# The second expert stage of a one-core language tower: from all eight experts of every token to the two chosen experts of each sequence

## The reference, cut to what matters

```python
def _L1_ffn_ref(x, Wr, br, W1, b1, W2, b2, gamma, beta):
    logits = jnp.mean(x, axis=1) @ Wr + br                # (64 sequences, 8 experts)
    routing_weights = jax.nn.softmax(logits, axis=-1)
    ...                                                   # scaled by capacity, softmax again
    top_w, top_i = jax.lax.top_k(rw_tok, 2)
    top_w = jax.nn.softmax(top_w, axis=-1)
    h = gelu(jnp.einsum('nd,edf->enf', xf, W1) + b1[:, None, :])      # 64 -> 128
    y = jnp.einsum('enf,efd->end', h, W2) + b2[:, None, :]            # 128 -> 64
    w_dense = jnp.zeros((N, E), x.dtype).at[jnp.arange(N)[:, None], top_i].add(top_w)
    out = jnp.einsum('ne,end->nd', w_dense, y).reshape(B, S, D)
    out = _layer_norm(out + x, gamma, beta)
```

## Time and profile before

| | before |
|---|---|
| median of 3 runs | 6802.49 us (6799.26 to 6812.74) |
| the profiled execution's own time | 6807.38 us |
| its span, first to last instruction | 6805.7 us |
| busy over the span: PE, DVE, ACT, POOL | 5514.7, 5229.1, 2711.6, 1975.4 us |
| granted TensorE clock, mean | 0.905 of full speed |

### The profile page before, as it was taken

The page is one execution under the profiler, slowest core; times in us unless marked ns, Lnnn a source line. Parts: engine busy times, 40 slices in busy tenths (PEclk is TensorE's granted clock), DMA queues, the critical chain, the costliest instruction groups (busy, mean ns, idle before and its releaser), DMA issues. The chain is left out here.

```text
span 6805.7 us, 109689 instructions
## 1 busy us (share of the span) xinstructions
PE 5514.7 (81%) x41602; PEld 3465.6 (51%) x41668; DVE 5229.1 (77%) x8911; ACT 2711.6 (40%) x4310; POOL 1975.4 (29%) x1937
## 2 busy tenths in 40 slices
PE   5659968958828999992399999999940989599998
PEld 3552256642215666662387878778830368433332
DVE  7878987877878888872288888888863577677776
ACT  3534433433425666661144444444420432233332
POOL 0010010010017830004777777777746010100000
PEclk8879989979969999995699999999975989699999
DMA  0000000002111000001122222222210000000001
GB/s 16 1 6 1 25 17 15 16 11 64 44 42 12 20 9 2 2 8 38 17 44 41 45 40 44 41 45 40 44 24 7 1 3 3 17 1 1 1 1 25
DMA packets 152318, 141.75 MB, mean 21 GB/s; under 512 B 71746, under 2 KB 136419, under 8 KB 150051
## 3 DMA queue, kind: packets, MB, share of 16 engines
q1 hardware_dynamic: 98462, 115.20, 5.8%
q0 software_dynamic: 53376, 20.06, 3.4%
q10 hardware_dynamic: 12, 0.39, 0.0%
HBM read 62.80 MB, written 38.09 MB: 15 GB/s over the span
## 5 line engine op out<-in xcount | busy, mean ns | idle before, releaser
L2888 PE MATMUL edges_bank<-part_room,hot_room 128*128 128x512 f32 x7168 | 1641.5, 391 | 223.5 <-DVE hot_room L2979 190.3
L2888 PEld LDWEIGHTS edges_bank<-part_room,hot_room 128*128 128x128 f32 x7168 | 1347.6, 188 | 517.4 <-issue 190.7
L2876 POOL DMA_INDIRECT XT<-gat_node_table,edges_idx x1152 | 1200.8, 1042 | 463.7 <-issue 460.7
L2909 ACT COPY XT<-edges_bank 128x512 f32<-128x512 f32 x896 | 524.0, 600 | 943.2 <-PE edges_bank L2888 939.4
L2997 DVE COPY_PREDICATED XT<-edges_tabs_p,XT 128x1024 f32<-128x1024 int32 (+3 forms) x896 | 632.9, 706 | 41.4 <-DVE edges_tabs_p L2971 7.4
L2979 DVE TENSOR_SCALAR hot_room<-edges_lanes,edges_nodes 128x512 fp32r<-128x512 f16 x896 | 395.1, 502 | 149.0 <-issue 73.1
L1005 ACT ACTIVATE expd_act_out<-expd_hp 128x1024 f32<-128x1024 f32 x256 | 262.2, 1024 | 525.9 <-PE expd_hp L927 525.9
L1041 DVE TENSOR_TENSOR expd_act_out<-expd_act_out,expd_h 128x1024 f32<-128x1024 f32 x256 | 312.7, 1221 | 185.9 <-ACT expd_act_out L1005 185.8
L1459 ACT ACTIVATE GT<-attc_sc,attc_nm 128x256 f32<-128x256 f32 x1024 | 400.4, 481 | 36.3 <-DVE attc_nm L1525 36.3
L1473 ACT ACTIVATE GT<-attc_sct 128x1024 f32<-128x1024 f32 x256 | 262.4, 1025 | 326.2 <-PE attc_sct L1393 325.5
L1524 DVE TENSOR_REDUCE attc_mx<-attc_sc 128x4 f32<-128x1024 f32 x256 | 313.3, 1224 | 86.9 <-PE attc_sc L1382 86.8
(11 more groups left out here) (774 smaller groups left out, 9895.6 us busy)
## 6 DMA issues: line engine op xcount, KB each, us to landing
edges_lanes<-gat_places SPq DMA_DIRECT2D x224, 128.0 KB, 3.1
gat_states<-GT SPq DMA_DIRECT2D x32, 768.0 KB
XT<-gat_node_table,edges_idx POOLq DMA_INDIRECT x1152
XT<-XT SPq DMA_DIRECT2D x32, 256.0 KB
XT<-XT SPq DMA_DIRECT2D x64, 128.0 KB
XT<-XT SPq DMA_DIRECT2D x128, 64.0 KB
gat_starts<-nodes_zeros SPq DMA_DIRECT2D x4, 1088.0 KB, 8.0
attb_q<-attb_rows SPq DMA_DIRECT2D x256, 2.0 KB
```

What stands on the lines that cost most here:

```text
L2876: nc.gpsimd.indirect_dma_start(out=rows[:, k, c, :], out_offset=None, in_=q.t_table, in_offset=bass.IndirectOffsetOnAxis(ap=idx[:, k, c:c ...
L2888: m = nc.tensor.matmul(banks[t % BANKS][:], hot[:, (k * GROUPS + j) % 2, b, t, :], parts[:, p, b].rearrange("p u c -> p (u c)"), start=b = ...
L2909: nc.scalar.copy(fetched[:, (k * GROUPS + j) % 2, t].rearrange("p u c -> p (u c)"), banks[t % BANKS][:]).then_inc(fetched_in, 1)
```

## The change

`route_sequences`, `ExpertTables` and `experts` are replaced in this block by one stage, `sequence_experts`. In "atta" SyncE builds a table in DRAM, `expert_pairs`, with a block of 128 rows of 384 floats for each ordered pair (a, c) of experts: W1 of a, W2 of a, W1 of c, W2 of c (12.6 MB, 48 DMAs of 256 KB, with rows of 512 bytes for W1 and 256 bytes for W2). In the new stage the router ends in an index for each sequence; GpSimd fetches 128 rows of 1536 bytes (196 KB) for one sequence with one indirect DMA, up to 6 sequences ahead. For each of 64 sequences TensorE does 4 hidden products of 128 columns, ScalarE two Gelus of 128 x 256, VectorE scales the two W2 by the weights (128 x 128), TensorE does 4 output products, ScalarE moves the sum with the mixed bias, TensorE turns it, and VectorE adds it to `X` (128 x 128). Two slots of the sort stand behind each scaling, so that the 125 are spent in 63 iterations.

The core of the diff:

```diff
-    with Stage(nc, "expb_in") as kept:
-        tables = ExpertTables(nc, kept, I["L1_ffn_W1"], I["L1_ffn_W2"], I["L1_ffn_b1"], I["L1_ffn_b2"])
-        route_sequences(nc, g, "routb", I["L1_ffn_Wr"], I["L1_ffn_br"], 8, ahead=tables)
-        experts(nc, g, "expb", tables, target=g.X, hide=HIDDEN["expb"])
+    sequence_experts(nc, g, "expb", pairs, I["L1_ffn_Wr"], I["L1_ffn_br"], I["L1_ffn_b1"], I["L1_ffn_b2"], g.X, HIDDEN["expb"])
...
+    def sync(self, sp):                                        # PairTable; called in attn0 ahead of the sort's slots
+        E = self.E
+        rows = self.table.rearrange("(a c p) (s f) -> a c p s f", a=E, c=E, s=2)
+        for e in range(E):
+            for half in range(2):
+                d = slice(half * D, half * D + D)
+                source = bc(self.W1[e], 1, E)
+                sp.dma_start(rows[e, :, d, 0, 0:P].rearrange("c d f -> d c f"), source).then_inc(self.built, 16)
+                sp.dma_start(rows[:, e, d, 1, 0:P].rearrange("a d f -> d a f"), source).then_inc(self.built, 16)
+            source = bc(self.W2[e], 1, E)
+            sp.dma_start(rows[e, :, :, 0, P:P + D].rearrange("c p f -> p c f"), source).then_inc(self.built, 16)
+            sp.dma_start(rows[:, e, :, 1, P:P + D].rearrange("a p f -> p a f"), source).then_inc(self.built, 16)
...
+                for b in range(B):                             # GpSimd, NB = 6
+                    if b >= NB:
+                        pool.wait_ge(used, b - NB + 1)
+                    nc.gpsimd.indirect_dma_start(
+                        out=chosen[:, b % NB, :], out_offset=None, in_=pairs.table,
+                        in_offset=bass.IndirectOffsetOnAxis(ap=idx[:, b:b + 1], axis=0)).then_inc(gathered[b % NB], 16)
...
+                for i in range(B + 3):                         # TensorE
+                    if i < B:
+                        hidden(i)
+                    if 0 <= i - 2 < B:
+                        out(i - 2)
+                    if 0 <= i - 3:
+                        turn_back(i - 3)
...
+                    for e in range(2):                         # ScalarE, hide_units
+                        m = nc.scalar.activation(hid[:, b % NH, e, :].rearrange("p (a t) -> p a t", a=TPB), hp[b % 2][:, :, e * P:(e + 1) * P], ACT.Gelu, bias=sel[:, e, b:b + 1])
...
+                    nc.scalar.activation(yT[:, b % 2, :], yp[b % 2][:, 0:P], ACT.Identity, bias=sel[:, 2, b:b + 1]).then_inc(y_moved, 1)
...
+                for i in range(B + 3):                         # VectorE, SLOT_RATE = 2
+                    if i < B:
+                        scale(i)
+                    while done < hide and done < (i + 1) * SLOT_RATE:
+                        g.order.vector(v)
+                        done += 1
+                    if 0 <= i - 3:
+                        add(i - 3)
```

More of the change, by code:

```diff
@@ L1090, in _, with attn0 @@
                 sp.wait_ge(stored, 64)
-def attn0(nc, g, I):
+def attn0(nc, g, I, pairs):
     scale = D ** -0.5
@@ L2109, in route_sequences, with sequence_experts @@
+def sequence_experts(nc, g, name, pairs, Wr, br, b1, b2, target, hide):
+    E = pairs.E
+    NB, NH = 6, 3
+    SLOT_RATE = -(-hide // B)
     capacity = float(-(-TOKENS * 5 // (4 * E)))
+    halves = [slice(0, D), slice(D, P)]
     with Stage(nc, name) as st:
         w, bias = st.sb("w", [P, E]), st.sb("bias", [B, E])
+        b1s, b2s = st.sb("b1", [E, P]), st.sb("b2", [E, 2, D])
+        rev = st.sb("rev", [B, E])
         mean = st.sb("mean", [P, B])
-        rw, load, hot, tmp, gt = (st.sb(n, [B, 1, E]) for n in ("rw", "load", "hot", "tmp", "gt"))
@@ L2114, in route_sequences @@
[L2114 to L2122, removed]
@@ L2123, in route_sequences @@
-        gates = GateSplit(nc, g, st, E, rest[:])
+        rw, load, tmp = (st.sb(n, [B, 1, E]) for n in ("rw", "load", "tmp"))
+        hots = st.sb("hots", [B, 3, E])
+        mx, rs, best1, best2, r1, r2, w2e = (st.sb(n, [B, 1]) for n in ("mx", "rs", "best1", "best2", "r1", "r2", "w2e"))
+        vals, diag = st.sb("vals", [B, 3]), st.sb("diag", [B, 3, B])
+        idx = st.sb("idx", [P, B], I32)
+        hotT, sel = st.sb("hotT", [E, 3, B]), st.sb("sel", [P, 3, B])
+        chosen = st.sb("chosen", [P, NB, PAIR])
@@ new lines, in sequence_experts @@
+        hid = st.sb("hid", [P, NH, 2, S])
+        yT = st.sb("yT", [P, 2, P])
+        spread, misc = st.ps("spread", [P, 3, B]), st.ps("misc", [P, 512])
+        small = misc[:, 0:2 * E].rearrange("p (n e) -> p n e", n=2)
+        turned_p = misc[0:E, 128:128 + 3 * B].rearrange("e (n b) -> e n b", n=3)
+        sel_p = misc[:, 320:320 + 3 * B]
+        hp = [st.ps(f"hp{n}", [P, 2, 512]) for n in range(2)]
+        yp, yt = [st.ps("yp", [P, 512]), misc], st.ps("yt", [P, 512])
+        names = ("loaded", "made", "own", "mean_ready", "product", "probs_ready", "shifted", "exped", "gap_ready", "gap_exped",
+                 "vals_ready", "spread_full", "hots_turned", "idx_ready", "hotT_ready", "sel_full", "sel_ready",
+                 "scaled", "hp_full", "hid_full", "used", "y_moved", "y_turned", "y_added")
@@ L2124, in route_sequences @@
+        (loaded, made, own, mean_ready, product, probs_ready, shifted, exped, gap_ready, gap_exped,
+         vals_ready, spread_full, hots_turned, idx_ready, hotT_ready, sel_full, sel_ready,
+         scaled, hp_full, hid_full, used, y_moved, y_turned, y_added) = (st.sem(n) for n in names)
+        gathered = [st.sem(f"gathered{n}") for n in range(NB)]
         with nc.Block() as block:
-            parts = {}
             @block.sync
             def _(sp):
-                sp.dma_start(w[0:D, :], Wr).then_inc(loaded, 16)
-                sp.dma_start(w[D:P, :], Wr).then_inc(loaded, 16)
+                for half in halves:
+                    sp.dma_start(w[half, :], Wr).then_inc(loaded, 16)
@@ L2131, in _ @@
                 sp.dma_start(bias[:], br.partition_broadcast(B)).then_inc(loaded, 16)
-                ahead.sync(sp)
+                sp.dma_start(b1s[:], b1).then_inc(loaded, 16)
+                for n in range(2):
+                    sp.dma_start(b2s[:, n, :], b2).then_inc(loaded, 16)
+                for _ in range(hide):
+                    g.order.sync(sp)
+            @block.gpsimd
+            def _(pool):
+                nc.gpsimd.iota(rev[:], pattern=[[-1, E]], base=E, channel_multiplier=0,
+                               allow_small_or_imprecise_dtypes=True).then_inc(made, 1)
+                pool.wait_ge(pairs.built, 16 * pairs.BUILDS)
+                pool.wait_ge(idx_ready, 1)
+                for b in range(B):
[4 more added lines that the diff above has]
+                        in_offset=bass.IndirectOffsetOnAxis(ap=idx[:, b:b + 1], axis=0)).then_inc(gathered[b % NB], 16)
@@ L2134, in _ @@
             @block.tensor
             def _(pe):
-                pe.wait_ge(loaded, 48)
+                pe.wait_ge(loaded, 96)
                 pe.wait_ge(mean_ready, 1)
@@ L2140, in _ @@
                 nc.tensor.matmul(small[0:B, 1, :], g.ones[0:B, 0:B], rw[:, 0, :], start=True, stop=True).then_inc(product, 1)
[L2141 to L2182, removed]
+                pe.wait_ge(vals_ready, 1)
+                nc.tensor.matmul(spread[:], g.ones[0:B, :], diag[:], start=True, stop=True).then_inc(spread_full, 1)
+                for n in range(3):
+                    m = nc.tensor.transpose(turned_p[:, n, :], hots[:, n, :], g.ident[0:B, 0:B])
+                m.then_inc(hots_turned, 1)
+                pe.wait_ge(hotT_ready, 1)
@@ new lines, in _, with hidden @@
+                nc.tensor.matmul(sel_p[:, 0:2 * B], b1s[:], hotT[:, 0:2, :], start=True, stop=True)
+                nc.tensor.matmul(sel_p[:, 2 * B:], b2s[:].rearrange("e n d -> e (n d)"), hotT[:, 2, :],
+                                 start=True, stop=True).then_inc(sel_full, 1)
+                def hidden(b):
+                    pe.wait_ge(gathered[b % NB], 16 * (b // NB + 1))
+                    if b >= 2:
+                        pe.wait_ge(hid_full, b - 1)
+                    for e in range(2):
+                        for a, half in enumerate(halves):
+                            m = nc.tensor.matmul(hp[b % 2][:, a, e * P:(e + 1) * P], chosen[half, b % NB, e * 3 * D:e * 3 * D + P],
+                                                 g.XT[half, b * P:(b + 1) * P], start=True, stop=True)
+                    m.then_inc(hp_full, 1)
@@ new lines, in out @@
+                def out(b):
+                    pe.wait_ge(hid_full, b + 1)
+                    pe.wait_ge(scaled, b + 1)
+                    if b == 0:
+                        pe.wait_ge(sel_ready, 1)
+                    if b >= 2:
+                        pe.wait_ge(y_moved, b - 1)
+                    for e in range(2):
+                        for a, half in enumerate(halves):
+                            m = nc.tensor.matmul(yp[b % 2][half, 0:P], chosen[:, b % NB, e * 3 * D + P:(e + 1) * 3 * D],
```

(35 more changed lines are left out.)

73 lines of the change are left out of this document (71 added, 2 removed).

## The result

| | before | after |
|---|---|---|
| median | 6802.4 us | 6650.8 us (6648.4 to 6655.5) |
| ratio to before | | 0.9775 (95% interval 0.9758 to 0.9792) |
| span of the profiled execution | 6805.7 us | 6648.0 us |

The changed kernel is 151.6 us faster; the forecast had 100.4, and its range ended at 132. In the two profiled executions the gain is 157.7 us.

What follows compares the result with a forecast made beforehand. VectorE was taken to bound the last expert stage, with SyncE's issuing as hidden second bound. Head, 289.0 us loop and 3 us end gave a 100.5 us gain: 6706.9 us profiled, 6702.0 us forecast, range 6670 to 6748 us.

Steps and rivals of the forecast that it cites:

- The sum: Whole kernel: the expert stage's 100.5 us gain carried to the end, 6706.9 us profiled, 6702.0 us as median.
- Part 1, the head: Expert stage from router to first scaling: narrower gate product, index and first gather, first scaling at 1501.5 us.
- Part 2, the loop: VectorE's loop in the expert stage: 103.0 outside exchanges, 160.3 + 11.7 for exchanges, 9 data, 5 gathers; 289.0 us.
- The rule by issues: Sort's 18 exchange bits: each takes the largest of SyncE's issues, issues-landing-merge, or VectorE's work; 160.3 us, plus 11.7 shortfall.
- The end: Behind the expert loop: the last sequence's products, move, turn and add, about 3 us, ending at 1793.5 us.
- Part 3: Other engines per 2.9 us iteration inside a row: TensorE 1.5 us, ScalarE 1.3 us, GpSimd's gather issue at worst 2.9.
- Part 4: Table build in "atta": 75 us at 167 GB/s against 213 us of cover, so it costs 0.
- DMA engines: Rival, expert stage: gathers and exchanges delay each other 2 us a bit more, 36 us, 6738 us; 10%.
- Half clock: Rival, expert stage: TensorE at half clock, handoffs of 0.5 us in 35.5 iterations, 18 us, 6720 us; 8%.
- GpSimd: Rival, expert stage: gather issues on GpSimd hold VectorE's slots in 35.5 iterations, 34 us, 6736 us; 4%.
- Table: Rival: table not ready when "atta" ends, delaying loads behind it; at 35 GB/s 6849 us; 5%.
- As much gain as work removed: Rival, expert stage: exchanges cost only VectorE's own work, 4.4 us a bit, loop 182 us, 6595 us; 1%.

Runs made afterwards that it cites:

- place 5419: The changed kernel with 146 idle wait instructions added on VectorE's stream ahead of the edge loop; 6675.7 us.
- 5555: The kernel before with 120 idle wait instructions added on VectorE's stream ahead of the edge loop; 6785.7 us.
- 5429: The changed kernel with 156 idle wait instructions added on VectorE's stream ahead of the edge loop; 6705.5 us, ratio 0.9849 to the kernel before.
- 5435: The kernel before itself, with no instructions added; 6802.4 us.

## Why the prediction was wrong

- **The sum** is the step that failed. "Sum. Against the profiled execution's own 6807.4 us ... 6706.9" carries the stage's gain to the kernel's end as if all behind it kept its length. The edge loop lost 41.2 us, since the change took 162 instructions out of VectorE's stream and so moved a loop body that, as I read the packets, had started just ahead of a border of the fetched pieces. The kernel before loses the same waits with 8 idle instructions added. No term and no rival of the forecast looked behind the stage; with the stage's own error alone the time would have been 6691.7. 6702.0 less these 41.2 and the stage's 10.3 is 6650.5; 6650.8 was measured. That they meet so closely is luck: the profiled gain has 1.5 us between the stages and 4.2 behind the edge loop more, neither explained, and the offsets of the two profiled executions happen to make up for them.
- **Part 1, the head**, right: first scaling at 1499.9 for 1501.5.
- **Part 2, the loop**, right in its mechanism, 11.5 us too long: 277.5 us (1499.9 to 1777.4) for 289.0. Outside the exchanges 103.9 us are left for the forecast 103.0. The three passes, from the first issue to the end of the last half-0 merge, took 50.7, 58.3 and 64.6, in all 173.6 us for 186.0. The rule by issues gives 160.3 of it and the gathers 4.1 (5 taken). For the rule's shortfall and the data's own time 9.2 us are left, where I took 11.7 and 9.
- **The end** took 5.9 us for 3, four adds behind a chain at the lower clock.
- **Part 3**, right that nothing but VectorE sets the pace, with less room than I gave it: TensorE 2.8 us an iteration, not 1.5, since at the lower clock its eight records of hidden products took 1.23 us where I had 0.61, and those of the output 1.12.
- **Part 4**, right: built in 51 us; the loads at 409.91 now stand at 407.70.
- **Rivals.** DMA engines: 5 us for the gathers, as taken, not 36. Half clock: it came, and cost at most the end's 2.9 us, not 18, since 2.8 us still fit into an iteration of 2.92; about 1.1 of the 2.9 went with the gathers. No run shows that rival's 0.5 us an iteration: at a granted clock of 0.50 TensorE's 2.8 us stayed 0.1 below the iteration, which VectorE set. GpSimd: the half slots took 684 and 688 ns beside gathers, 683 before, so no hold. Table: not late. As much gain as work removed: no, 94.7 us of waiting say so.

With the loop body moved by 24 in the kernel before, 6761.8 us, the change itself is worth about 110 us; the other 41 came with it by chance and can go the same way.

## What to carry to other kernels

Here 162 instructions fewer ahead of a hardware loop with a body of 275 came with a loop 41.2 us shorter, and 8 idle ones more in the kernel before with one 40.5 us shorter. In a kernel with such a loop, look for idle time without a releaser that occurs once a round, for packets on the instruction queue inside the loop, and repeat the measurement with a few idle instructions added before a gain or loss is given to an edit. A count of issues by SyncE's issue time foretold the exchange-bound stretches to 8% here (160.3 us of 173.6); work that is taken from in between turns into waiting, and a second issuing queue gave back 32 us of it here.

## What the runs showed of the hardware that I had not expected

- With VectorE's loop of 275 instructions at four of ten starting places, q14 had 5 packets of 8 KB in each round, at the other six none. The loops with packets took longer over 14 jumps: against the same kernel without packets about 11 from place 5419, 13 from 5555, 37 from 5429 and 40 to 41 from 5435. That these packets are the loop's own instructions is my reading.
- Idle wait instructions in a row were not free: VectorE stood 5.5 us behind 96 of them, 8.2 behind 120, 12.4 behind 160 and 13.2 behind 168, for nothing that the profile shows.
- DRAM to DRAM in rows of 512 and 256 bytes ran at 249 GB/s with the engines 95% busy, faster than the 167 GB/s that I had from loads to SBUF.
- An issue took ScalarE's queue 699 ns in the median, SyncE's 590.
